# First stream's tail in quarter projections; attention's second key tile cleared last, maxima ten steps ahead

## What is computed

```python
x = x + 0.5 * _L0_ffn_ref(_layernorm(x, axis=-1), L0_ffn_Wr, L0_ffn_We)
x = x + _L0_attn_ref(_layernorm(x, axis=-1), Wq, bq, Wk, bk, Wv, bv, Wo, bo)
x = x + 0.5 * _L0_ffn_ref(_layernorm(x, axis=-1), L0_ffn_Wr, L0_ffn_We)
# in the attention, for every head:
attn = jnp.einsum('bhsd,bhtd->bhst', q, k)     # q, k rotated by position, q scaled
attn = jax.nn.softmax(attn, axis=-1)
out = jnp.einsum('bhst,bhtd->bhsd', attn, v)
```

## Time and profile before

| | |
|---|---|
| runs | 6196.45, 6199.58, 6208.9 us; median 6199.58 |
| profiled execution | 6194.03 us, span 6192.2 us |
| TensorE busy | 6120.4 us, 99% of the span |
| VectorE busy | 5907.1 us, 95% |
| ScalarE busy | 4872.4 us, 79% |
| GpSimd busy | 457.0 us, 7% |
| first stream | 0 to 637 us |
| attention | 638 to about 5725 us |

### The profile page before, as it was taken

The page is one execution under the profiler, slowest core; times in us unless marked ns, Lnnn a source line. Parts: engine busy times, 40 slices in busy tenths (PEclk is TensorE's granted clock), DMA queues, the critical chain, the costliest instruction groups (busy, mean ns, idle before and its releaser), DMA issues. The chain is left out here.

```text
span 6192.2 us, 161079 instructions
## 1 busy us (share of the span) xinstructions
PE 6120.4 (99%) x54380; PEld 2730.9 (44%) x54380; DVE 5907.1 (95%) x7028; ACT 4872.4 (79%) x9032; POOL 457.0 (7%) x635
## 2 busy tenths in 40 slices
PE   8998999999999999999999999999999999999999
PEld 6887333333333333333333333333333333333787
DVE  7998999999999999999999999999999999995787
ACT  4453688888888888888888888888888888887222
POOL 3444100000000000000000000000000000000332
PEclk9999899999999999999999999999999999999999
DMA  2335101010101001010101010101000101000111
GB/s 85 125 119 133 33 14 18 14 18 14 18 14 18 14 14 17 14 18 15 18 14 18 14 18 15 18 14 18 14 15 14 18 14 18 7 23 22 57 55 35
DMA packets 135459, 178.79 MB, mean 29 GB/s; under 512 B 71488, under 2 KB 97120, under 8 KB 131552
## 3 DMA queue, kind: packets, MB, share of 16 engines
q1 hardware_dynamic: 134752, 169.30, 12.0%
HBM read 98.47 MB, written 70.78 MB: 27 GB/s over the span
## 5 line engine op out<-in xcount | busy, mean ns | idle before, releaser
L1238 DVE TENSOR_REDUCE at_mx<-at_m 128x1 f32<-128x1024 f32 x4060 | 4966.6, 1223 | 30.4 <-PE at_m L1078 9.5
L1201 ACT ACTIVATE at_ex<-at_s 128x512 f32<-128x512 f32 x6144 | 3444.2, 596 | 465.5 <-PE at_s L1103 61.3
L1078 PE MATMUL at_m<-at_k,at_q 48*128 48x512 f32 x8104 | 2951.6, 443 | 0.0
L1103 PE MATMUL at_s<-at_q,at_k 50*128 50x512 f32 x6144 | 2399.0, 445 | 5.5 <-ACT at_ex L1201 5.5
L1112 PE MATMUL at_s<-at_ex,at_v 128*32 128x256 f32 x24576 | 1964.3, 391 | 0.0
L1078 PEld LDWEIGHTS at_m<-at_k,at_q 48*128 48x128 f32 x8104 | 1193.9, 185 | 1672.0 <-DVE at_mx L1238 1650.8
L1201 ACT ACTIVATE at_ex<-at_po 128x512 f32<-128x512 f32 x2048 | 1219.7, 596 | 143.1 <-PE at_po L1103 5.6
L1103 PEld LDWEIGHTS at_s<-at_q,at_k 50*128 50x128 f32 x6144 | 981.0, 185 | 22.7 <-ACT at_ex L1201 12.4
L1112 PEld LDWEIGHTS at_s<-at_ex,at_v 128*32 128x32 f32 x24576 | 483.5, 108 | 1114.9 <-ACT at_ex L1201 1112.2
L1103 PE MATMUL at_po<-at_q,at_k 50*128 50x512 f32 x2048 | 907.8, 443 | 0.0
L1112 PE MATMUL at_po<-at_ex,at_v 128*32 128x256 f32 x8232 | 662.1, 394 | 0.8 <-issue 0.8
(11 more groups left out here) (236 smaller groups left out, 3465.5 us busy)
## 6 DMA issues: line engine op xcount, KB each, us to landing
at_q<-q_parts SPq DMA_DIRECT2D x96, 256.0 KB, 5.4
at_k<-k_parts SPq DMA_DIRECT2D x96, 256.0 KB, 6.1
q_parts<-fr_parts SPq DMA_DIRECT2D x64, 256.0 KB, 2.2
k_parts<-fr_parts SPq DMA_DIRECT2D x64, 256.0 KB, 2.4
attended<-at_o SPq DMA_DIRECT2D x512, 17.0 KB
fr_x<-in_x SPq DMA_DIRECT2D x16, 512.0 KB, 4.4
after_ffn<-fr_acc SPq DMA_DIRECT2D x16, 512.0 KB, 3.0
v_by_head<-fr_v SPq DMA_DIRECT2D x16, 512.0 KB, 3.7
```

The source lines that it names most:

```text
L1078: ins = pe.matmul(pm[w][:, h * GT:(h + 1) * GT], Q[p][rows, base + i * P:base + (i + 1) * P], K[p][rows, c * CW + h * GT:c * CW + (h + 1) ...
L1103: pe.matmul(banks[SCORE[sb_][t]], K[p][rows, j * P:(j + 1) * P], Q[p][rows, sb_ * QU:(sb_ + 1) * QU], start=True, stop=True).then_inc(s_s, 1)
L1201: ac.activation(Ex[j % NX][w][:, :], banks[SCORE[sb_][t]], ACT.Exp).then_inc(s_e, 1)
L1238: ve.tensor_reduce(out=mx[u][:, i, c:c + 1], in_=first[(k - AHEAD + 2) % len(first)][:, 0:CW] if opens else pm[w][:, :], op=ALU.max, axis= ...
```

## The change

In the first stream's tail the rotary and the value projections of the last group are each issued in two halves, with opening products between the halves; one more product runs before the transposes, and the third pair of banks is used from product 6 on instead of 9. The arithmetic and the number of matmuls are the same. In the attention phase AHEAD goes from 12 to 10, so two products fewer run before the first unit, and the last unit but one has two more steps with a product. GpSimd clears the value tiles and sets the ones first, copies the first values, and only then clears `K[1]`; the counts of `s_one` that TensorE and SyncE wait for follow (2 and 4).

```diff
--- before.py
+++ after.py
@@ -226,7 +226,7 @@
         pz = first[1][:, GT:2 * GT]
         pT = [first[2][:, c * GT:(c + 1) * GT] for c in range(NC)]
         pq = [ps(f"pq{k}", 1) for k in range(2)]
-        LATE = 9
+        LATE = 6
         FIRST = [n % 2 if n < LATE else (n - LATE + 2) % 3 for n in range(RED)]
         pl, pp = pz[:, 0:TG * E], pz[:, D:D + TG * E]
 
@@ -373,29 +373,33 @@
                                                  start=(t == 0 and c == 0), stop=(t == len(SPLIT) - 1 and c == NC - 1))
                         last.then_inc(s_mm, 1)
 
-                def rotary(n, w):
-
-                    if w == 0:
-                        need(pe, s_xl[1], n + 1)
-                        need(pe, s_vc, n)
-                    else:
-                        need(pe, s_qe, n * 2 + 1)
-                    for h in range(2):
+                def rotary(n, w, halves=(0, 1)):
+
+                    if halves[0] == 0:
+                        if w == 0:
+                            need(pe, s_xl[1], n + 1)
+                            need(pe, s_vc, n)
+                        else:
+                            need(pe, s_qe, n * 2 + 1)
+                    for h in halves:
                         for t, (a, b) in enumerate(SPLIT):
                             for c in range(NC):
                                 last = pe.matmul(pq[h][:, :], (wqh, wql)[b][:, c, 2 * w + h, :], (xh, xl)[a][1][0][:, c, :],
                                                  start=(t == 0 and c == 0), stop=(t == len(SPLIT) - 1 and c == NC - 1))
-                    last.then_inc(s_qk, 1)
-
-                def values(n):
-                    need(pe, s_qe, n * 2 + 2)
-                    for i in range(TG):
+                    if halves[-1] == 1:
+                        last.then_inc(s_qk, 1)
+
+                def values(n, first=0, end=TG):
+                    if first == 0:
+                        need(pe, s_qe, n * 2 + 2)
+                    for i in range(first, end):
                         for t, (a, b) in enumerate(SPLIT):
                             for c in range(NC):
                                 last = pe.matmul(pq[i // 2][:, (i % 2) * D:(i % 2 + 1) * D],
                                                  (xh, xl)[a][1][0][:, c, i * P:(i + 1) * P], (wvh, wvl)[b][:, c, :],
                                                  start=(t == 0 and c == 0), stop=(t == len(SPLIT) - 1 and c == NC - 1))
-                    last.then_inc(s_v, 1)
+                    if end == TG:
+                        last.then_inc(s_v, 1)
 
                 pe.wait_ge(s_c, 4 * DMA)
                 turn(0, 0)
@@ -421,15 +425,21 @@
 
                     opening_products(0, 2)
                     values(n - 1)
-                    opening_products(2, 3)
+                    opening_products(2, 4)
                     turn(1, n)
-                    opening_products(3, 12)
-                    rotary(n, 0)
-                    opening_products(12, 16)
-                    rotary(n, 1)
-                    opening_products(16, 20)
-                    values(n)
-                    opening_products(20, RED)
+                    opening_products(4, 9)
+                    rotary(n, 0, (0,))
+                    opening_products(9, 11)
+                    rotary(n, 0, (1,))
+                    opening_products(11, 14)
+                    rotary(n, 1, (0,))
+                    opening_products(14, 16)
+                    rotary(n, 1, (1,))
+                    opening_products(16, 19)
+                    values(n, 0, 2)
+                    opening_products(19, 21)
+                    values(n, 2)
+                    opening_products(21, RED)
 
                 def body(g, u, it):
                     here, after, before_, older = (runs(g, d) for d in (0, 1, -1, -2))
@@ -884,7 +894,7 @@
     COPY_AT = 2 * LAG
     HQ = QU // 2
     E0 = 8
-    AHEAD = 12
+    AHEAD = 10
     W = 32
     CH = 3
     LOAD_AT = 6
@@ -983,7 +993,7 @@
                     hold(sp, s_mq, v * (4 * DMA) + 4 * DMA, s_tick)
 
                 rows_of_max(0, 0, 0)
-                hold(sp, s_one, 2, s_tick)
+                hold(sp, s_one, 4, s_tick)
 
                 def pair(r, k, n, more):
                     for sb_ in range(SB):
@@ -1020,26 +1030,27 @@
 
             @block.gpsimd
             def _(gp):
-                for w in range(2):
-                    gp.memset(K[1][HALF * w + BL:HALF * (w + 1), :].bitcast(F32), 1.0).then_inc(s_one, 1)
-                    gp.wait_ge(s_one, w + 1)
                 for p in range(NB):
                     gp.memset(V[p][:, :, :, :], 0.0)
                 for j in range(NX - LAG, NX):
                     for w in range(2):
                         last = gp.memset(Ex[j][w][:, :], 1.0)
                 last.then_inc(s_one, 1)
-                gp.wait_ge(s_one, 3)
+                gp.wait_ge(s_one, 1)
                 for p in range(NB):
                     last = gp.memset(V[p][:, :, :, HD:HD + 1], 1.0)
                 last.then_inc(s_one, 1)
-                gp.wait_ge(s_one, 4)
+                gp.wait_ge(s_one, 2)
 
                 def fill(p, n):
                     hold(gp, s_lv[p], n * (2 * DMA) + 2 * DMA, s_tick)
                     gp.tensor_copy(V[p][:, :, :, 0:HD], vst[p][:, :, :, :]).then_inc(s_vh, 1)
 
                 fill(0, 0)
+                gp.wait_ge(s_vh, 1)
+                for w in range(2):
+                    gp.memset(K[1][HALF * w + BL:HALF * (w + 1), :].bitcast(F32), 1.0).then_inc(s_one, 1)
+                    gp.wait_ge(s_one, w + 3)
 
                 def pair(r, k, n, more):
                     if more:
@@ -1134,7 +1145,7 @@
                     if n >= len(first):
                         pe.wait_ge(s_mr, 2 + RED + n - len(first) + 1)
                     max_products(pe, first[(n - AHEAD + 2) % len(first)], Q[0], K[0], QU, n).then_inc(s_m, 1)
-                pe.wait_ge(s_one, 4)
+                pe.wait_ge(s_one, 2)
                 times_v(banks[FROM[0]], 1, KT - 1, True, False)
 
                 def pair(r, k, n, more):
```

## The result

The changed kernel took 6279.68 us (median of 4 runs, 6267.55 to 6285.69); the kernel before, in 4 runs of its own, 6204.24. The ratio is 1.0124 [1.0113, 1.0136]: slower by 75 us where 5 were forecast, and outside the range. The profiled execution took 6281.48 us (span 6279.7, mean granted clock 0.984), 87.5 us more than the profiled one of before (6194.03, 0.992).

What follows compares the result with a forecast made beforehand. TensorE was taken to set the steady pace, its waits at unit heads being lost for good. Tail, opening, clock and phase end made -9.1 us, steady state +14: +4.9, so 6204.5 us against 6199.58, range 6190 to 6224.

Steps and rivals of the forecast that it cites:

- the seven units: Attention units v = 10, 26, ..., 106: an instruction packet delays the maxima's write, late by 1.5 to 2.0 us each, 12 us.
- The other units: Attention units v = 5, 21, ... lose 0.1 to 0.2 us each and v = 13, 29, ... 0.1: 2 us.
- The tail: End of the first stream: halved projections and an earlier third bank start the next stage sooner, -5.9 us.
- Rival 4: First stream's tail: SyncE's chained stores hold the stage's end, so the tail gives nothing; 6210.4 us, chance 0.02.
- The opening's steps: Start of the attention phase: shorter first cast, two opening products fewer, key memsets hidden; -3.9 us.
- the +0.4 us for the clock: First attention steps at 1.2 GHz: an earlier start may meet the clock's rise differently, between 0 and +1.5 us.
- The margin: Head of every attention unit: 6.27 us left for a 6.0 us round trip of the maxima; steady state +14 us.
- rival 2: Unit heads: ordinary units late too; at 0.5 us beyond the margin +20 us, 6224 us; chance 0.13.
- rival 3: Unit heads: late groups v = 8 and 13 keep their delay, late by 1.1 to 2.0 us, 6215.5 us; chance 0.14.
- rivals 1: Unit heads: no instruction packet meets the write, 6193.5 us; chance 0.20.
- Rival 5: Unit heads: each ordinary round trip grows to two full fixed costs, late by 0.4 us, +45, 6250 us; chance 0.03.
- The likeliest case: Whole kernel: tail and opening gains, seven late units in the steady state; 6198 to 6212 us, chance 0.48.

Runs made afterwards that it cites:

- two reads: Changed kernel, ten ahead, with the rows of maxima written in reading order so two reads replace four: 6193.31 us, ratio 0.9991.
- the padded one: Changed kernel with 50 further semaphore instructions at the very start of TensorE's program: 6343.49 us, ratio 1.0212.
- two trips: Kernel before, twelve ahead; in v = 10, 26, ... SyncE first writes the row twice to spare memory, waiting each time: 6227.73 us, ratio 1.0044.
- three trips: Kernel before, twelve ahead; in v = 10, 26, ... SyncE first writes the row three times to spare memory, waiting each time: 6265.76 us, ratio 1.0101.

## Why the prediction was wrong

In short: the waits at the heads of the seven units came as forecast, 12.3 us in all for 12. The step that failed is the price of such a wait. The prediction took it at its own length; the clock that fell behind six of the seven made it 53 us. The other units, costed at 2 us, lost 35 more.

**The tail was right in size, in part by luck.** -5.2 us for -5.9. The last maximum ended at 627.05 where 628.7 was forecast, the first quarter opened a pause of 1.69 us as worked out (1.7), and the second and the later ones none. What failed here is the 1.23 us "from the last end to GpSimd's first instruction of the next stage". In both traces the begin lies 3.0 to 3.2 us behind the landing of SyncE's last stores (635.0 to 638.00, 629.6 to 632.78), and VectorE's end was only near it by chance: over all ten profiled executions the begin is 2.9 to 3.2 us behind that landing and 1.2 to 5.8 behind VectorE's end. That another chain would be late next was seen; that it already set the time in the kernel before was not. Rival 4 named it, but took it to stand still. A second error made up for the first: the stores landed at 629.6 where 630.9 was forecast, since TensorE was back at full clock for the second quarter, which ended at 602.5 and not 603.7, and GpSimd started at 604.05.

**The opening's steps were right, the clock was not.** The cast took 0.94 us, the first step came 13.0 us after the begin (12.8 forecast) and the key memsets hid. But the +0.4 us for the clock were about +4: the low stretch did not end a little sooner or later, it took in 19.6 us of steps instead of 10.9. The bound of 1.5 us was too narrow as well; the row that it came from the earlier trace rows is one execution. From the first step on, the low stretch took 6 to 28 us in the ten profiled executions, 6 with two reads, whose program up to there differs only in these reads and their write, and 25.8 with the memsets alone. So the 4 us are those of one execution, and not shown to be the change's.

**The margin: the right units, the wrong price.** This is the term that decided, and "late by 1.5 to 2.0 us, 7 times, 12 us" the step in it that failed. The arithmetic of slack held: units with no packet within 2 us of the issue, nor one of 8 KB on the reads (v mod 16 = 1, 2, 6, 14), are 0.05 to 0.07 us late, so 6.27 us do suffice for 6.0, and rival 2 did not occur. Packets moved with TensorE's program as worked out, v = 8 and 13 lost their long delay, so rival 3 did not occur, and v = 10, 26, ... came into the costly place, with waits of 1.3 to 2.1 us where 1.5 to 2.0 were forecast. The sum took such a wait at its face value: 7 times 1.7 is 12 us. Measured were 50.5, 7.2 us each, since the clock fell behind six of the seven: 12.3 us of waits, and 92 us at low clock, of which 40 are lost.

Over the kernel as changed, the kernel before with ten ahead and the padded one there are 33 waits for the rows from 0.88 us up. None of the five up to 1.07 us was followed by a low clock, of the 14 from 1.18 to 1.59 eleven were, of the 14 from 1.70 to 2.12 thirteen. The length doesn't decide alone: none of the seven with two trips was, at 1.22 to 1.65. Nor does a fall need ten ahead or a wait for these rows. In all ten profiled executions TensorE stands for 1.59 to 1.89 us near the end of the phase, and in eight the clock fell behind it. The trace of before has this case, and it should have raised the question (TensorE's timeline, then the stretch behind it, columns as in the earlier trace rows):

```profile
5596.47 0.50 PE L1103 MATMUL at_s<-at_q,at_k 50*128 50x512 f32 x1 [1.67 <-ACT at_ex L1201]
```
```profile
5597.90:5601.30 3.40, 3.40 (x24) 0.90 (x20) 1.97 (x2) 2.17 (x4) 0.00 (x0) 0.50 0.02 5
```

The 0.52 of 655 to 666 in the earlier trace rows was another hint, behind an opening in which TensorE had mostly waited for VectorE. The price of a low step stood there as well: 2.16 us for 1.23, so each 10 us at low clock cost 4.3. The Trainium skill (TensorE: Matmul & The Clock Gate, HAM oscillation) describes a kernel that falls back to the half clock at each wait for a DMA and pays for it every time. The trace shows the same kind of loss, but from shorter waits than that kernel's 3 to 5 us, here 1.2 to 2.1, and not behind every one of them.

**What was left out.** The other 105 units were to lose 2 us and lost 34.7. Half of it is in v = 3, 7, 11, 15 and so on (0.50 to 0.71 us each, 15.8 in all). There a packet of 8 KB, of the other instruction queue, lies 5.4 us behind the issue, when the last of the four reads is on its way. Unit 23, its timeline and the queues of 1567.4 to 1567.7 us:

```profile
1563.66 3.23 SPq L989 DMA_DIRECT2D at_q<-max_rows  x4
1568.95 0.49 PE L1089 MATMUL at_m<-at_k,at_q 48*128 48x512 f32 x1 [0.52 <-DMA at_q<-max_rows]
```
```profile
q14 instruction: 1, 0.01, 11.5%
```

The reads are issued in time, by 1566.9, and yet TensorE waits 0.52. In the kernel before the same packet lay at 7.85 us, behind the landing, and cost nothing. In v = 0, 4, 8, 12 such a packet is 0.50 us behind the issue and the reads start after 1.8 to 2.1 us (7.4 us in all); in v = 5 and 13 TensorE's own lies 0.3 us ahead of it (9.6, where 2 were forecast). I had listed the packets of one queue of two, and watched only the write; the reads' landing is as exposed. That these packets are the cause is read from their places alone: no run moved them separately. With two steps or 2 us of slack more no unit of these waits.

**Neither the end of the phase** (+0.3) **nor rivals 1, 4 and 5** mattered. Rival 5 took the fixed cost of the Trainium skill (DMA: Bandwidth & Descriptors, Anatomy of one DMA) twice; that section is about DMAs that GpSimd issues, these are SyncE's, and the ordinary write kept its 1.6 us. The likeliest case had the late units and their waits right, left out the clock behind them, and so was short by a factor of four in its largest term; neither the range nor a rival had a case for that.

**Open.** Why a low stretch lasts 3.4 us once and 41 another time behind waits of like size. Why no wait of the two-trip run was followed by a fall. And the fall at 5600 to 5770 us, at the end of ScalarE's loop, where TensorE stands for 1.6 to 1.9 us: 3.4 us long in the profile of before, 10.2 in that of after, 27 with the maxima twelve ahead again, 34 with the memsets alone, none with two reads or three trips. At 4.3 us for each 10 it and the low clock of the opening could account for much of the spread of 12 to 27 us among the runs of a kernel without late units; only the profiled executions show them. No run tried to remove it.

## What to carry to other kernels

A margin that recurs must be counted against the slowest case of its chain, with every kind of packet that can fall on any of its landings, not against the ordinary one. On TensorE a wait of over a microsecond can cost far more than its own length: where the clock falls it costs several times that (here 7 us for 1.8), so slack of one or two microseconds in front of it is cheap, and it can be had by shortening the chain (two reads for four) as well as by starting earlier. When a change shortens a program or shifts an issue by two steps, instruction packets come to lie elsewhere; look where they lie before and work out where they will lie.

## What the runs showed of the hardware

- One wait of 1.2 to 2.1 us, in a TensorE otherwise busy to 98%, is often followed by half its clock, for 3.4 to 41 us: 24 of 28 waits for rows in the three kernels that lost by it, but none of seven in the run with two trips.
- An instruction packet of 16 KB from 0.4 to 1.4 us behind the issue of a 16 KB write makes its landing 1 to 2 us later, though the DMA engines are busy to only 9% (700 to 5200 us of the changed kernel). The write in the other layout, 2.2 us long, was not made later by it. Fifty instructions in front of a loop moved the packets some 2.5 us earlier, and made the kernel 1% slower than the changed one.
- Four reads whose pieces lie scattered in memory take SyncE 3.2 us to issue, two with long rows 0.7.
- After the last landing of the first stream 2.9 to 3.2 us pass until GpSimd starts the attention phase, in all ten profiled executions.
